# Merging two lists of work at another pace: a factor of 0.65 becomes 0.75

## The reference

```
x = x + layernorm(attn(layernorm(x)))          # linear attention, 8 heads of 64
x = x + layernorm(ffn(layernorm(x)))           # 16 routed experts, 2 shared

attn:  q, k, v = h @ Wq, h @ Wk, h @ Wv
       q = softmax over a head's 64 features, scaled;  k = softmax over the tokens
       context = k^T v (per head);  out = (q context) @ Wo + bo
ffn:   s = softmax(u @ centroids^T);  g = the two largest of 16, the others 0
       u + sum_e g_e * (u @ Wr_e^T + br_e) + (u @ (Ws_0 + Ws_1)^T + sum bs) / 2
```

## Time and the profile before

| | us |
|---|---|
| median of 8 runs | 3138.29 |
| lowest and highest of the 8 | 3114.59, 3466.36 |
| the profiled execution, its own time | 3114.59 |
| its span on the slowest core (core 7) | 3112.7 |
| spans of all cores | 3097.3 to 3112.7 |
| TensorE busy | 2456.6 (79%) |
| VectorE busy | 1577.6 (51%) |
| ScalarE busy | 113.0 (4%) |

### The profile page before, as it was taken

One profiled execution on the slowest core, in us unless ns is written; L12 is line 12 of the kernel. 1 busy time (PEld: TensorE's weight loads), 2 busy tenths in 40 slices (PEclk: granted clock), 3 DMA queues, 4 the chain that ended last, 5 costly groups with the idle time before them and its releaser, 6 DMA issues.

```text
span 3112.7 us, 38404 instructions; the slowest of 8 cores (3097.3 to 3112.7 us)
## 1 busy us (share of the span) xinstructions
PE 2456.6 (79%) x12014; PEld 1111.5 (36%) x12014; DVE 1577.6 (51%) x2882; ACT 113.0 (4%) x353; POOL 15.8 (1%) x29
## 2 busy tenths in 40 slices
PE   3252521449999999499999994999999949999995
PEld 1121210114444444234444441344444414444442
DVE  4133322666656644566666445666664454444445
ACT  0000000000000000000000000000000000000000
POOL 0000000000000000000000000000000000000000
PEclk9666765669999999799999997999999979999997
DMA  5988997123334433424344434233433342333334
GB/s 109 136 129 155 137 131 137 49 68 75 67 90 103 102 75 75 142 76 96 67 102 102 78 76 144 71 97 67 101 82 80 75 143 55 78 75 79 76 76 133
DMA packets 673683, 296.31 MB, mean 95 GB/s; under 512 B 631857, under 2 KB 634929, under 8 KB 672340
## 3 DMA queue, kind: packets, MB, share of 16 engines
q1 hardware_dynamic: 668308, 251.86, 33.8%
q0 software_dynamic: 5184, 42.01, 11.5%
HBM read 142.78 MB, written 79.69 MB: 71 GB/s over the span
## 4 chain that ended last, share of the span: by engine, by line
PE 65%; DVE 11%; DMA 9%; DVEq 6%; issue 4%; another core or an unknown queue 3%; SPq 1%; ACT 0%; POOL 0%; ACTq 0%; POOLq 0%
PE pb L882 56%; DMA xA<-xin 8%; PE pb L827 2%; PE pb L785 2%; DVEq L416 2%; PE pb L871 2%; SPq L79 1%; DVE att L527 1%; DVEq L64 1%; DVE ftmp L628 1%; DMA cen_st<-cen 1%; DVEq L524 1%; DVE Dbn L414 1%; PE pbT L839 1%
## 5 line engine op out<-in xcount | busy, mean ns | idle before, releaser
L882 PE MATMUL pb<-wrt,uT 128*128 128x512 bf16 x9216 | 2019.0, 380 | 0.9 <-issue 0.2
L882 PEld LDWEIGHTS pb<-wrt,uT 128*128 128x128 bf16 x9216 | 895.9, 98 | 1071.8 <-issue 9.5
L602 DVE SCALAR_TENSOR_TENSOR racc<-pb,gAll,racc 128x512 f32<-128x512 f32 x1024 | 758.3, 750 | 836.1 <-PE pb L882 811.1
L732 PE MATMUL pbT<-eye,hb 128*128 128x128 bf16 x256 | 32.1, 306 | 218.4 <-DVEq L64 218.0
L602 DVE SCALAR_TENSOR_TENSOR racc<-pb,halfc,racc 128x512 f32<-128x512 f32 x128 | 96.1, 751 | 124.9 <-PE pb L882 124.9
L785 PE MATMUL pb<-wqb,hT 128*128 128x512 bf16 x256 | 70.0, 428 | 78.4 <-DMA hT<-hscr 78.4
L732 PEld LDWEIGHTS pbT<-eye,hb 128*128 128x128 bf16 x256 | 24.8, 137 | 224.5 <-issue 224.3
L414 DVE BATCH_NORM_STATS2 Abn<-xA 128x6 f32<-128x512 f32 x32 | 22.2, 693 | 136.7 <-DMA xA<-xin 133.4
L839 PE MATMUL pbT<-eye,ub 128*128 128x128 bf16 x256 | 23.6, 247 | 81.9 <-DVEq L64 81.7
L871 PE MATMUL pb<-eyeblk,uT 128*128 128x512 bf16 x256 | 77.7, 433 | 0.0
L453 DVE CAST vb<-pb 128x512 bf16<-128x512 f32 x32 | 22.2, 694 | 109.2 <-PE pb L759 84.3
(11 more groups left out here) (107 smaller groups left out, 940.4 us busy)
## 6 DMA issues: line engine op xcount, KB each, us to landing
xA<-xin SPq DMA_DIRECT2D x128, 256.0 KB, 5.7
wbf<-wr POOLq DMA_DIRECT2D x16, 2048.0 KB, 37.1
wrt<-wbf SPq DMA_TRANSPOSE x1152, 2.8
yscr<-att SPq DMA_DIRECT2D x32, 512.0 KB, 3.5
yld<-yscr SPq DMA_DIRECT2D x32, 512.0 KB, 3.9
out<-ftmp SPq DMA_DIRECT2D x32, 512.0 KB, 2.9
hscr<-hT SPq DMA_DIRECT2D x32, 256.0 KB, 38.1
hT<-hscr SPq DMA_DIRECT2D x32, 256.0 KB, 4.7
```

What stands on the lines that cost most here:

```text
L602: ii = v.scalar_tensor_tensor(rsl, pb[bk][:], gcol, rsl, ALU.mult, ALU.add)
L732: last = pe.transpose(pT[:, kk * P:(kk + 1) * P], hb4[i4][:, kk * P:(kk + 1) * P], eye[:])
L882: last = pe.matmul(pb[bk][:], uT[:, kk * NTOK + tt * P:kk * NTOK + (tt + 1) * P], wrt[par][:, kk * HID:(kk + 1) * HID], start=(kk == 0), s ...
```

## The change

One factor in `prop_merge`. It multiplies the count to which the second list is advanced after each attention item:

```
             outl.append(la[ia])
-            want = int(round((ia + 1) * ratio * 0.65))
+            want = int(round((ia + 1) * ratio * 0.75))
             while ib < want:
                 outl.append(lb[ib]); ib += 1
```

## The result

The changed kernel took 3093.44 us (median of 11 runs, 3081.08 to 3360.66), the kernel before on the same chips 3137.79 (median of 32). The ratio is 0.9871, with a 95% interval of 0.9848 to 0.9894: 33 to 48 us less. The forecast was 3104, -34.4. In some executions one die ran at a lower granted clock; they are left out of every ratio, and where no undisturbed profile was to be had (0.95, and experiment 9), only the cores or the stretch that it left alone are used.

A forecast was written before the change was run, and what follows sets the result against it. PE bounds the tails and nearly the mixed parts (45.75 us idle), with DVE the limit between projection and `ub`. Terms -23.9 - 8.7 - 6.8 + 5 = -34.4 us from 3138.3 give 3104, range 3078 to 3140.

The forecast's parts named there:

- Cover for `ub`: More expert groups between second output projection and first `ub` transpose cut PE's waits from 28.1 to 4.2 us: -23.9 us.
- The doubt of 0.3 us more for each lone evacuation: Lower bound at `ub`: 24 added DVE evacuations might each cost a further 0.3 us gap, 7 us less gain.
- Cover for the gates: One more group ahead of the second gate transpose in eight of twelve pairs removes PE waits: -8.7 us of 13.0.
- Clock: Half-rate dips in the mixed parts, 13.6 us costing 6.8 us of work, vanish with the `ub` waits: -6.8 us.
- Starts: At the second and third mixed window's start `o2` begins five us later; 2.5 us cost each, +5 us.
- The 1.1 us that I added to 1.4 for a late rise of the clock: At each of two window starts, PE's later continuous work may delay the clock's rise; 2.5 us taken each.
- DMA: SyncE queue: the pair's 5.2 us block overruns 4.4 us free per unit by 0.8, absorbed by next slack; cost nothing.
- rival D: Weights come late as SyncE's slack can't fit the pair's 5.2 us block; slower, up to +28 us; chance 0.08.
- C: PE's wait moves from `ub` to bank evacuation, `qT` or gates; -15 us, no measurable change; chance 0.22.
- B: All 45.75 us of mixed-part idle and 6.8 us of clock go, starts cost nothing; -53 us, 3086; chance 0.12.
- The sum: Whole kernel: -23.9 - 8.7 - 6.8 + 5 = -34.4 us, giving 3104 from the median.

The follow-up runs named there:

- 0.95: Factor 0.95 in place of the kernel before's 0.65; windows 1 to 3 took 1768.2 us on cores 4 to 7, ratio 0.979.
- experiment 9: Changed kernel (0.75) with the pair's block of eight transfers split into two halves on the SyncE queue; windows 1 to 3 took 1785.0 us against 1789.0.
- experiment 1: Kernel before, still reaching 65%, with the `ub` cover of 0.75 paid for by other places; windows 1 to 3 took 1810.2 us, ratio 0.9965.
- experiment 8: Kernel before (0.65) without each tile's residual add ahead of the second layernorm; windows 1 to 3 took 1795.4 us against 1826.6.
- experiment 2: Kernel before, reaching 75%, with the closing part at the old pace and `ub` meant to keep its 0.65 cover; windows 1 to 3 1804.7 us, ratio 0.9947.
- experiment 4: Changed kernel (0.75) with the pair's eight transfers issued by GpSimd instead of SyncE; windows 1 to 3 took 1818.9 us against 1789.0.
- 0.85: Factor 0.85 in place of the kernel before's 0.65; windows 1 to 3 took 1771.3 us, ratio 0.9807.
- experiment 7: Factor 0.85 with the closing items kept at the pace of 0.65; windows 1 to 3 took 1772.9 us against 1771.3.

## Why the prediction was right, step by step

**Cover for `ub`: right.** -25.0 against -23.9, with 3.2 us in five waits left where I named 4.2. The places came out less well than the sum, and that is luck: tiles 8/9 keep 0.1 us instead of 1.7, 18/19 0.4 instead of 1.2 and 26/27 0.5 instead of 0.8, while the three other pairs (10/11, 16/17, 24/25) keep 2.3 together instead of 0.5. The mechanism is shown from both sides: more PE work there (experiment 1, 2.4 us left) and less DVE work there (8, 2.9 us left) remove the same waits at 0.65. The doubt of 0.3 us more for each lone evacuation, 7 us in all, didn't show in the sum.

**Cover for the gates: right.** -8.4 against -8.7, 13 waits down to 5, where eight of twelve pairs were to lose theirs. Experiment 2 bears the count out by pairs: where its order has five groups between the first gates and the second transpose, no wait is left, and where it has three, each pair waits.

**Clock: right, a little low.** -8.5 against -6.8. I had read two stretches of one core and guessed the third; the cores' mean was 17.5 us at the 1.2 GHz level instead of 13.6. That a dip goes with such a wait is borne out: half-rate time was 0.4 us after, 0.9 in experiment 8 without touching the pace, and 24.3 in experiment 4, which has long weight waits in place of those at `ub`.

**Starts: the step that was mis-sized, and its working left out the longest wait.** I gave +5 for two; these two measured +2.1 and -0.4, with +0.4 for the first. `o2` did start 5 us later on average, as I had worked out, and its wait shrank, from 10.9 to 7.2 us over the cores. But this was not idle time saved: the waits for `qn` ahead of it, which the working doesn't name, grew from 29 to 34 us in each of the two starts. In sum PE's idle time rose by 1.3 and 0.7 us; the rest of the delay is the two bias groups that now run earlier. The 1.1 us that I added to 1.4 for a late rise of the clock did not show: the last rise came 4.0 us later in the second and 1.2 us earlier in the third start, and half-rate time was 49.1 and 51.2 us before, 49.5 and 49.5 after. The sign holds at 0.75: experiment 2, which has the closing part at the old pace there, has these two starts 0.9 and 0.6 us shorter than the kernel after. At 0.85 the closing part at the same factor gains about 2 us at each start (experiment 7).

**DMA: the cost that I set to nothing was 4.0 us.** I let a block of 5.2 us overrun a slack of 4.4 us and put the 0.8 us into the next unit's slack. The queue is not only issue: the set behind the block also has to land before the unit's first matmul, 2.8 us in the median of windows 1 to 3 and 5.8 us at the wait shown in experiment 9. The landing stands in rival D, but not in the working of this term. So rival D was there, at 4.0 / 12 = 0.33 us a pair, far from the 2.9 us at which it would have eaten the gain. Experiment 9 shows that the block is the cause: half of it, and the wait is gone.

**The rivals.** C, the wait that moves to banks or gates, showed 0.8 us at banks and no more; in experiment 1, where elsewhere loses cover, it is what ate the gain. B, all idle gone and the starts free, is about what 0.85 brings (-55.3 against its -53), though by other terms: there the starts, which B leaves as they are, gave 8, and waits for weights took 7. At 0.75 ten waits stay, as the counts of their places had it.

**The sum.** The missed terms (starts 3 too dear, weights 4 too cheap, clock and `qn` 3 too small) nearly cancel, so the total is better than its parts, and that is luck. The ratio stands for some 40 us less, windows 1 to 3 for 37.6. The difference lies within the ratio's interval. In the two profiled executions the first pass differs the other way, by 4.9 us, and doesn't explain it.

## What to carry to other kernels

When two lists share in-order engines, look for each step that crosses from the matrix engine to the vector engine and back, subtract the durations of what both do between the two waits, and give that step as many independent groups as the difference asks, counted in the order as it is built; a global pace gives it to all steps at once, and is worth trying well beyond the first gain. After shortening a unit of work, lay the whole set of its transfers, issue and landing, into the new length, and split any block of other transfers that the queue must pass between two sets.

## What was unexpected

- Transposing transfers lost speed when plain transfers, issued by GpSimd, ran at the same time: median landing 5.8 us for those that overlapped, against 3.9 at 0.75 and 2.8 for the rest, up to 12.0 in the rows shown, and 24.5 us of waits on PE instead of 4.0 (experiment 4). With the half-rate time that these waits bring, moving the block to an idle engine cost 30 us.
- The first pass, with no change in it, took 505.0 us on average in one execution and 509.9 in another, with cores from 495.9 to 531.4 us in the latter, while windows 1 to 3 agree within 0.5% over the cores in both. The time of a whole execution blurs an effect of 20 us that the stage shows plainly.
